# Two additions of the scan's MLP tail put into TensorE's accumulation and moved by ScalarE

## The reference, cut to what matters

```python
x0 = _rmsnorm(x, rms1_w)
x1 = _mamba(x0, ...)              # scan over 16 states, gate, out_proj
x = x1 + x
x2 = _rmsnorm(x, rms2_w)
x3 = relu(relu(x2 @ fc1.T + b1) @ fc2.T + b2) @ fc3.T + b3
return x + x3                     # and the block's result is added to its input
```

## Time and profile before

| | us |
|---|---|
| median of 3 runs (lowest, highest) | 1642.82 (1642.12, 1642.84) |
| profiled execution | 1651.1 |
| its span | 1649.3 |
| scan with posts of chunks 0 to 6 | 527.4 to 927 |
| granted TensorE clock, mean | 0.924 |

### The profile page before, as it was taken

How to read it: one execution, slowest core, us unless ns; L and a number is a source line. 1 busy time by engine, 2 the same in 40 slices (tenths; PEclk the granted TensorE clock), 3 DMA queues, 4 the chain that set the end, 5 groups by cost and what they waited for, 6 DMA issues and landing times.

```text
span 1649.3 us, 23216 instructions
## 1 busy us (share of the span) xinstructions
PE 1344.1 (81%) x8006; PEld 723.1 (44%) x8022; DVE 1229.9 (75%) x1782; ACT 1027.4 (62%) x1726; POOL 924.1 (56%) x484
## 2 busy tenths in 40 slices
PE   6748068666947888887888788999999999999987
PEld 2316057532312333333333345555555555555553
DVE  2973135338679999999999778888888888888862
ACT  4423034368844555555455378888888888888863
POOL 0440633300388888888798366555555566666640
PEclk9877589879779999999999999999999999999999
DMA  2005421120032222223342021111111111111100
GB/s 65 0 1 81 144 64 52 58 56 0 10 87 79 77 73 68 77 68 99 117 138 71 22 46 40 33 40 33 40 33 40 33 40 33 46 40 33 40 20 26
DMA packets 67689, 87.49 MB, mean 53 GB/s; under 512 B 12611, under 2 KB 34293, under 8 KB 67317
## 3 DMA queue, kind: packets, MB, share of 16 engines
q1 hardware_dynamic: 65268, 81.28, 18.5%
q0 software_dynamic: 2304, 4.74, 0.9%
HBM read 53.18 MB, written 9.74 MB: 38 GB/s over the span
## 4 chain that ended last, share of the span: by engine, by line
PE 41%; DVE 13%; ACT 8%; issue 5%; POOL 4%; DMA 0%; DVEq 0%; another core or an unknown queue 0%; POOLq 0%; SPq 0%; ACTq 0%
DVE ssm_state L1311 7%; PE at_two L1637 6%; PE glu_bank L1573 5%; PE ssm_bank L980 4%; PE at_one L1733 4%; ACT home_dt L1842 4%; DVE ssm_seen L1325 4%; PE glu_bank L1554 4%; PE at_two L1615 3%; PE at_two L1667 3%; PE at_one L1645 3%; POOL ssm_dbu L1205 2%; PE glu_bank L1599 2%; POOL ssm_seen L1214 2%; PE ssm_bank L1013 1%
## 5 line engine op out<-in xcount | busy, mean ns | idle before, releaser
L1852 POOL TENSOR_TENSOR at_direct<-at_direct,home_u 128x1024 f32<-128x1024 f32 x64 | 151.0, 2359 | 270.4 <-DVE home_u L1943 270.4
L1205 POOL TENSOR_TENSOR ssm_dbu<-ssm_dtu,ssm_b_all 128x1024 f32<-128x1024 f32 x128 | 298.0, 2359 | 0.1
L980 PE MATMUL ssm_bank<-ssm_seen,ident 128*128 128x512 f32 x512 | 257.6, 628 | 44.4 <-POOL ssm_seen L1214 42.4
L1122 ACT ACTIVATE ssm_bank<-home_dt,ssm_decay 128x512 f32<-128x512 f32 x256 | 174.8, 690 | 139.3 <-DVE ssm_state L1311 138.5
L980 PEld LDWEIGHTS ssm_bank<-ssm_seen,ident 128*128 128x128 f32 x512 | 99.5, 199 | 146.9 <-issue 81.1
L1311 DVE TENSOR_TENSOR_SCAN ssm_state<-ssm_bank,ssm_dbu 128x512 f32<-128x512 f32 x128 | 148.6, 1205 | 19.9 <-POOL ssm_dbu L1205 16.1
L1311 DVE TENSOR_TENSOR_SCAN ssm_state<-ssm_bank,ssm_carry,ssm_dbu 128x512 f32<-128x512 f32 x128 | 156.1, 1265 | 5.3 <-POOL ssm_dbu L1205 2.8
L1857 POOL TENSOR_TENSOR home_z<-home_z,at_inv 128x1024 f32<-128x1024 f32 x64 | 121.5, 1899 | 19.7 <-DVE at_inv L1954 19.7
L1637 PE MATMUL at_two<-home_u,at_hs 128*128 128x512 f32 x256 | 125.5, 613 | 7.4 <-ACT at_kT L1780 5.4
L1863 POOL TENSOR_TENSOR at_direct<-at_direct,at_rnorm 128x1024 f32<-128x1024 f32 x64 | 121.9, 1905 | 0.2
L1980 DVE TENSOR_REDUCE at_peak<-at_scores 128x8 f32<-128x1024 f32 x64 | 78.1, 1221 | 58.6 <-PE at_scores L1700 47.2
(11 more groups left out here) (238 smaller groups left out, 3177.2 us busy)
## 6 DMA issues: line engine op xcount, KB each, us to landing
ssm_b_all<-ssm_b_rows SPq DMA_DIRECT2D x128, 256.0 KB, 3.1
at_v_mix<-at_v SPq DMA_DIRECT2D x112, 128.0 KB, 2.3
at_hs<-branch SPq DMA_DIRECT2D x64, 128.0 KB, 2.3
moe_w<-in_moe_w SPq DMA_DIRECT2D x16, 256.0 KB
moe_to_experts<-moe_empty SPq DMA_DIRECT2D x10, 258.0 KB, 7.7
moe_slot_rows<-moe_to_experts SPq DMA_DIRECT2D x10, 258.0 KB, 2.9
x<-in_x SPq DMA_DIRECT2D x8, 256.0 KB, 3.6
moe_rows<-moe_from_experts SPq DMA_DIRECT2D x8, 256.0 KB, 5.4
```

The lines of the kernel that those rows point to most:

```text
L980: last = nc.tensor.matmul(bank[Y0 + half][:], ident[:], seen[:, n % 2, half], start=False, stop=n == STATES - 1)
L1122: nc.scalar.activation(bank[DA0 + half][:], chunk_of(dt[:, half], t), ACT.Exp, scale=decay[:, half, n:n + 1]).then_inc(r[f"da{half}"], 1)
L1205: nc.gpsimd.tensor_tensor(dbu[:, i % RING], dtu[:, t % 2], b_all[:, i % B_RING:i % B_RING + 1, :].broadcast_to([P, 2, CH]), ALU.mult).then ...
L1852: nc.gpsimd.tensor_tensor(direct[:, n % TURNED], direct[:, n % TURNED], crossed[n % 2], ALU.add).then_inc(s["added"], 1)
```

## The change

`branch` and `x` are no longer added by VectorE and GpSimd. Each is multiplied by the identity matrix on TensorE and accumulated in bank W0 behind the product to which it belongs. ScalarE moves the sums out: it squares `out` + branch straight from the bank, copies it into `branch`, and writes `down` + x + branch with the bias into `x`. Square moves from place 2 to place 1, and ScalarE's wait is now for TensorE. VectorE's multiplication at place 3 also waits for `branch`.

```diff
@@ TensorE, posted(i, 0)
                     for half in range(2):
-                        last = nc.tensor.matmul(bank[W0][:], out_w[:, half], chunk_of(z[:, half], t),
-                                                start=half == 0, stop=half == 1)
-                    last.then_inc(r["out"], 1)
+                        nc.tensor.matmul(bank[W0][:], out_w[:, half], chunk_of(z[:, half], t),
+                                         start=half == 0, stop=False)
+                    nc.tensor.matmul(bank[W0][:], ident[:], chunk_of(branch, t), start=False, stop=True
+                                     ).then_inc(r["out"], 1)
@@ TensorE, posted(i, 10)
                     for c in range(2):
-                        last = nc.tensor.matmul(bank[W0][:], fc3[:, c], chunk_of(z[:, c], t),
-                                                start=c == 0, stop=c == 1)
-                    last.then_inc(r["down"], 1)
+                        nc.tensor.matmul(bank[W0][:], fc3[:, c], chunk_of(z[:, c], t),
+                                         start=c == 0, stop=False)
+                    nc.tensor.matmul(bank[W0][:], ident[:], chunk_of(x, t), start=False, stop=False)
+                    nc.tensor.matmul(bank[W0][:], ident[:], chunk_of(branch, t), start=False, stop=True
+                                     ).then_inc(r["down"], 1)
@@ ScalarE
-                t = posted(i, 2)
+                t = posted(i, 1)
                 if t is not None:
-                    act.wait_ge(r["branch"], up_to(t))
-                    nc.scalar.activation(chunk_of(dt[:, 0], t), chunk_of(branch, t), ACT.Square
+                    act.wait_ge(r["out"], up_to(t))
+                    nc.scalar.activation(chunk_of(dt[:, 0], t), bank[W0][:], ACT.Square
                                          ).then_inc(r["squared"], 1)
+                    nc.scalar.activation(chunk_of(branch, t), bank[W0][:], ACT.Copy).then_inc(r["branch"], 1)
...
+                t = posted(i, 11)
+                if t is not None:
+                    act.wait_ge(r["down"], up_to(t))
+                    nc.scalar.activation(chunk_of(x, t), bank[W0][:], ACT.Identity, bias=mlp_b[:, 4:5]
+                                         ).then_inc(r["x"], 1)
@@ GpSimd
-                t = posted(i, 4)
-                if t is not None:
-                    pool.wait_ge(r["branch"], up_to(t))
-                    nc.gpsimd.tensor_tensor(chunk_of(x, t), chunk_of(x, t), chunk_of(branch, t), ALU.add
-                                            ).then_inc(r["joined"], 1)
@@ VectorE, posted(i, 3), posted(i, 10), posted(i, -1)
                     dve.wait_ge(r["rstd"], up_to(t))
+                    dve.wait_ge(r["branch"], up_to(t))
...
-                t = posted(i, 10)
-                if t is not None:
-                    dve.wait_ge(r["down"], up_to(t))
-                    dve.wait_ge(r["joined"], up_to(t))
-                    nc.vector.scalar_tensor_tensor(chunk_of(x, t), bank[W0][:], mlp_b[:, 4:5], chunk_of(x, t),
-                                                   ALU.add, ALU.add).then_inc(r["x"], 1)
...
-                t = posted(i, -1)
-                if t is not None:
-                    dve.wait_ge(r["out"], up_to(t))
-                    nc.vector.tensor_tensor(chunk_of(branch, t), chunk_of(branch, t), bank[W0][:], ALU.add
-                                            ).then_inc(r["branch"], 1)
```

More of the change, by code:

```diff
@@ L751 @@
 SCAN = ("dtu c c_all da0 da1 dbu state0 state1 carried seen seen_apart y gated out branch "
-        "weights fc3 fc1_folded squared power logged rstd normed joined up hidden0 half hidden1 down x "
+        "weights fc3 fc1_folded squared power logged rstd normed up hidden0 half hidden1 down x "
         "centred spread_squared variance spread_logged rooted ready operands")
```

## The result

The changed kernel takes 1633.46 us (median of 5 runs; the kernel before beside it 1642.12): ratio 0.9943, 95% interval 0.9929 to 0.9958, so 9.4 us faster (6.9 to 11.7). The forecast was 5.8 us.

A forecast was written before the change was run, and what follows sets the result against it. VectorE, 93% busy, was taken as nearly the bound in the scan, TensorE's chain in the tail. Posts -10.8 and tail +2.6 gave -8.2 us; +2.4 for remaining low clock gave -5.8, 1637 us; range 1632 to 1646.

The forecast's parts named there:

- the case that was called the likeliest: Whole kernel: a third of five low clock stretches at the join stay; -5.8 us, 1637 us (-3.3 to -7), chance 0.42.
- rival B: Scan: TensorE's clock never falls at the join of x and branch; -8.2 us, 1634.6 us, chance 0.16.
- `out`: Behind the `out` product: ScalarE's in-order wait takes back VectorE's saving; 0 a chunk, +0.6 us for t=0.
- The join: GpSimd's addition of x and branch at place 4: without it, GpSimd's next products and `seen` come 1.2 us sooner.
- The clock: TensorE's low clock at the joins of t=1 to 5: a third of five stretches stay, 2.4 of 7.2 us.
- `down`: Two products behind `down` delay C: net +0.43 us in chunks scanning from carried state, +0.63 in the others (plain).
- What comes behind: TensorE's 2.03 us gap behind `down` (t=0, 2, 4) shrinks to about 1; VectorE's 1.0 us wait is won three times.
- The tail: Chunk 7, beside the attention: the new products lie on TensorE's chain of waits and cost +2.6 us in full.
- Rival C: Scan: TensorE becomes the bound if VectorE's holes for C exceed 1.25 us a chunk; +11.9 us, 1654.7 us, chance 0.10.
- Rival A: Scan: the clock goes on falling at every join; -1.0 us, 1641.8 us, chance 0.22 with its surroundings.

The follow-up runs named there:

- e1: Kernel before with only the half at `out`: TensorE adds branch, ScalarE squares and copies it, VectorE's addition there gone; ratio 0.9984.
- e2: Kernel before with only the half at `down`: TensorE adds x and branch, ScalarE's Identity moves the sum, GpSimd's join gone; ratio 0.9920.
- e5: Changed kernel with ScalarE's Copy of branch at place 2 instead of 1; ratio 0.9943 to the kernel before.
- e3: Changed kernel, but GpSimd again joins x and branch at place 4 and TensorE adds only x behind `down`; ratio 0.9963 to the kernel before.
- e4: Kernel before with one edit: GpSimd's addition of x and branch stands at place 8 instead of 4; ratio 0.9911.
- e9: Kernel before plus two unread identity products a chunk (chunks 0 to 6) in TensorE's idle time before its wait at place 7; ratio 0.9939.
- e11: Chunks 0 to 6 as e7, chunk 7 as in the kernel before; 1631.33 us against 1653.01 for the kernel before, ratio 0.9875.
- e7: Changed kernel, but GpSimd joins x and branch at place 8 and TensorE adds only x behind `down`; ratio 0.9925 to the kernel before.

## Why the prediction was right, and where it was not

The sign and the range held, but not by the case that was called the likeliest: the time lies below that case's own range (1635.5 to 1639.5). What happened is rival B, the clock never falls, which had a chance of 0.16 and for which -8.2 stood there. Its part in the posts was -10.8, measured -10.1. That this was no luck of the total shows chunk by chunk. From one `out` to the next, before against changed (first profiles):

| us | forecast for B | measured |
|---|---|---|
| t=0 | -1.1 | -0.8 |
| t=2, 4, each | -2.55 | -2.6 |
| t=1, 3, 5, each | -1.7 | -1.5 |
| t=6 | +0.5 | +0.35 |

Posts and tail together make -7.3 us (-10.1 and +2.8, see below), within the interval of the whole (6.9 to 11.7) but near its end; no run places the 2 us that are left.

- `out`: forecast 0 but for t=0. e1 has the sum about so: 400.1 against 400.0 and 400.2; in the changed kernel the half at `out` costs 1.2 us (e2), 0.6 of them in chunk 0. The value was about right, the reason was half of it. I gave ScalarE's order alone. The trace after has two holes in each chunk, 0.30 for ScalarE's exponential and one before `seen` for C, which stands behind the new product (0.26 in carried chunks, 0.50 in plain ones, 0.86 for t=0). e5 takes the first away in four of seven chunks and wins 0.3 us in all. So ScalarE's order explains only part of why nothing was won at `out`.
- The join: forecast to matter most, and it did (e3, e4). GpSimd's holes 8.7 to 0.3.
- The clock: this is the term that was mis-sized. "I expect a third of them to stay" put 2.4 us on five low stretches; none of the eight stayed, in neither profile. TensorE's gap at the join is now 1.53 us in carried chunks and 1.79 in plain ones (forecast 1.5 to 2). e9 prices them: six stretches fewer, with two products a chunk added and nothing else changed, 7.4 us, 1.2 us each; forecast 7.2 for five, 1.4 each.
- `down`: forecast a hole of 1.1 in carried and 1.3 in plain chunks. Measured seven, 9.0 us in all, 1.19 in carried and 1.43 in plain chunks. Its net cost was forecast as +0.43 and +0.63. e2 and e4 differ by the two products, ScalarE's Identity, L1291 and the join; in chunks 1 to 5, where neither has a low stretch behind `down`, e2 takes 0.65 us more in carried and 0.87 in plain chunks.
- What comes behind: the gap of 2.03 became 1.21 (forecast about 1), the low stretches there went, and with them the 1.01 us at the scan. e3 shows this step by itself: five low stretches at the join, none behind `down`, where one product was added. But the longer burst was not the only way: in e9 and e4 the gap behind `down` is 2.03 to 2.04 us as before, and with the low stretches of the join gone, those behind `down` in chunks 2 and 4 went too.
- The tail: forecast +2.6. It can't be had from single profiles: 47.4 and 50.4 for the kernel before. The one with as much low clock (6.8 us) as both of the changed kernel is 47.4, against 50.3 and 50.1: +2.8. e9 and e4, whose chunk 7 has the same additions on the same engines as before, have 47.6 with the same 6.8 us, and e1, with the product at `out` alone, has 48.4. e11, which leaves chunk 7 as it was, has 45.8, with 3.4.

Rival C, TensorE as the bound, did not come, though the sign that the prediction gave for it did: VectorE's holes for C are 12.1 us in seven chunks (9.0 and 3.1), 1.7 a chunk and more than the 1.25 at which C was to decide. 5.4 us of such holes were there before, so the change added 6.7, less than the 8.75 us that it took off VectorE, and the join and the clock gave more. The threshold should have been set on the holes added. Rival A, the clock falling at every join, is what e3 shows for chunks 1 to 5. Another sign was set too high: TensorE's busy time in the posts rose 5 us, where 20 were forecast with chunk 7, since the 18 us of new products stand against others that no longer run at half the clock. VectorE's fell 9, forecast 10 with chunk 7.

Still open: the 2.6 us of e1, why the time changed by more than the posts in e3, and what decides whether the clock falls after a gap of 2.03 or 2.77 us.

## What to carry to other kernels

Ask of an addition that is to be moved not only what its engine is busy with but what stands behind it in the order there: here a 1.26 us addition stood in a stretch in which GpSimd was late, and four places later it was free. Before moving work to another engine, try moving it along its own; the one-number edit (e4) was worth more than the change. Products put at the end of a long burst delay the small one behind, on which the next engine waits (e7: one such product less a chunk is 5.7 us).

## What the runs showed of the hardware that I had not expected

Two products a chunk into a bank that nobody reads (e9) made the kernel faster, 0.9939. TensorE's gaps of 2.8 to 3.0 us ahead of its wait at the join became 1.1 to 1.3, and its product there ran at 2.4 GHz.

In the kernel before, the clock fell at three places behind a gap of 2.03 us and at five behind gaps of 2.77 or 3.01, but not after 2.77 at 550.41 nor after 2.04 at 915.70. The second profile has the eight falls at the same places of the work, 2 us earlier, as all of that stage. In the posts of all 13 profiles it never fell behind a gap of 1.92 us or less (the changed kernel has none above 1.79). Behind gaps of 2.03 or 2.04 us it fell 12 times and did not 8 times; behind 2.75 to 2.79 us it fell 8 times and did not 4 times, all four in chunk 0; behind 3.00 to 3.02 us it fell each of 12 times. So the length of the gap alone does not say whether it falls.
